# Gated-delta group loop and mixture of experts: diagonal blocks gathered by ACT, whole-tile transposes, the last two norms ahead of the group border, routing weights split by expert

## The chip, the core and the metric

The kernel runs on one core of one Trainium2 chip, in one launch. The metric is the device time of that launch in microseconds, the median of several runs. Five engines work side by side, each through its own list of instructions in order, and wait for one another only at semaphores: PE (TensorE, matmuls), DVE (VectorE), ACT (ScalarE), POOL (GpSimd) and SP (which only issues DMA).

## The reference, cut to what matters

The reference is a two-layer network on `x` of shape (4, 256, 256): per layer a gated mixer and a mixture of experts (MoE), each added to `x`. The change touches the delta-rule attention of the first layer and the way in which the MoE weighs its experts. For each head of the attention a strictly lower triangular matrix is built, the unit triangular system is solved, and the output is normalized and gated:

```python
diff = jnp.where(lower, g[..., :, None] - g[..., None, :], 0.0)
decay = jnp.where(lower, jnp.exp(diff), 0.0)
A = jnp.where(strict, -(k_beta @ jnp.swapaxes(k, -1, -2)) * decay, 0.0)
attn = jax.scipy.linalg.solve_triangular(eyeC - A, eyeC, lower=True, unit_diagonal=True)
...
out = core * jax.lax.rsqrt(jnp.mean(core * core, -1, keepdims=True) + EPS) * norm_w
out = out * jax.nn.silu(z.astype(jnp.float32))
return out.reshape(Bb, Ss, VAL_DIM) @ w_out
```

The first MoE has 64 experts with 64 hidden units each, of which a token takes 6, and one shared expert; the second has 8 experts with 256 hidden units, of which a token takes 2:

```python
h = relu2(jnp.einsum('th,eih->tei', x, w1)) * w_dense[:, :, None]
routed = jnp.einsum('tei,ehi->th', h, w2)
```

## The kernel before

Five phases follow one another: a front phase (gates), `delta_phase`, `moe_phase` 0, a small mixer, `moe_phase` 1. All tokens (1024) lie along the free dimension.

`delta_phase` works through 8 groups (`NG`) of 2 key heads and 4 value heads. `groups` writes group 0 and group 7 out and runs groups 1 to 6 in a hardware loop (`Fori`), on each engine. In what follows g0 is the first group. Nothing but the order of the code and the semaphores decides what runs when; there is no scheduler. One group is, on PE:

1. The border. `gram(g, 0)`, then `rms(g - 1, 6)`, `gram(g, 1)`, `rms(g - 1, 7)`: products of keys and queries of the new group, with the last two norm sums of the group before between them. The matmul of `rms` (L469) goes to ACT's `root` (Ln L797, then Exp L799), then DVE's `normalize` (L970), then POOL's multiply (L1091). The first `gram` waits for the sixth `normalize`.
2. The m stage. Eight steps n of `gram` (L487, L488) and `decay` (L499 to L504). ACT takes the decays into one of two buffers `dec` (L786, L787), DVE multiplies them into `m` (L986, L990). `output` (L477, pairs of matmuls of the group before) is done one pair a step from n = 4 on, the rest behind.
3. `gate` (L518), `turn_v` (L512), and four `project_qk` (L445) of the next group, as cover. Meanwhile DVE copies and transposes the 32x32 diagonal blocks of `m` into `mt`, in four instructions of 32 partitions each (L1002), inverts all blocks by 31 steps of substitution (L1016, L1021), with `add_output` (L950) in between, and then transposes the inverse `inv` into two layouts, `t64` (`untransposed`, L1026) and `pT` (`transposed`, L1031), in seven instructions of 32 partitions. `tr_ready` counts them.
4. `below32` (L526) and `merge32` (L537, L539) build the 64x64 inverses from the 32x32 ones, with ACT's evictions (L849, L854 to L856) between; `filler(4)` is a projection (L445) that waits for the first `convolve` (L942) of DVE, which stands behind the transposes; then the step to 128 (`below64`, `merge64`: L546, L550), `solve` and `cross` (L555, L561).
5. The mix stage. Eight steps of `mix` (L570, L572), `project_v` (L445) and `rms`; two of them also hold `k_norm` (L462), the norm of the next group's keys, which ACT's `root_k` takes (L765).

In `moe_phase` the hidden units are worked in units of 128 by 512: PE `hidden` (L1475), ACT relu, POOL square, PE `weights` (L1485, L1487: spreads the routing weight of an expert over the rows of its hidden units), DVE multiply (L1453), PE `second` (L1495). The routing weights are split in three bf16 parts, so that 3 x 64 = 192 rows do not fit in the 128 rows of one matmul: in MoE 0 `weights` is two matmuls, of 128 rows (parts 0 and 1, `wTa`) and of 64 rows (part 2, `wTb`). DVE also works in these stretches on gates that are needed later (`late_gates`).

## Time and profile before

| | |
|---|---|
| median of 3 runs | 1879.65 us (1879.03 to 1881.52) |
| profiled execution, its own time | 1879.69 us |
| its span, first to last instruction | 1877.8 us |
| mean granted TensorE clock | 0.919 |
| PE busy, share of the span | 1549.9 us, 83% |
| DVE busy, share of the span | 1216.3 us, 65% |
| ACT busy, share of the span | 767.8 us, 41% |
| POOL busy, share of the span | 331.8 us, 18% |

So 1.9 us lie outside the span. Busy times are sums over stages with different limits; what counts at a place is which wait ends last there. The granted clock is 1.0 at 2.4 GHz and 0.5 at 1.2 GHz.

### The profile page before, as it was taken

To read this page: it belongs to the slowest core of one execution; us is meant where nothing else is said; L and a number is where in the kernel's file an instruction comes from. 1 tells how busy PE (TensorE), PEld (TensorE's weight loads), DVE (VectorE), ACT (ScalarE), POOL (GpSimd) and SP (SyncE) were. 2 spreads that over 40 slices of the span, in tenths; PEclk is the share of its full clock that TensorE was granted. 3 is DMA by queue.
4 is the path that set the end of the run, shared out by engine and by line. 5 is a ranking of instruction groups with operands and counts; after the bars stand their busy time and mean duration, and the time that the engine had idled before them with its cause. 6 is when DMAs were issued, how large, how long until landed. Compare 5 with 4: busy or idle time off the path is not lost. (4 is left out here: it accounts for less than half of the span.)

```text
span 1877.8 us, 24845 instructions
## 1 busy us (share of the span) xinstructions
PE 1549.9 (83%) x8568; PEld 870.9 (46%) x8568; DVE 1216.3 (65%) x2045; ACT 767.8 (41%) x1576; POOL 331.8 (18%) x289
## 2 busy tenths in 40 slices
PE   0117869889879889888898898897799999989998
PEld 0113456456447447446446446546433333334433
DVE  6977776785696696596597597585276665632211
ACT  2214545556546555455555564555321111120111
POOL 6110003102102201300300300300322232200222
PEclk9968979979889988898898997997899999989999
DMA  1010000000000000000000000000200111010010
GB/s 56 0 47 23 12 13 13 22 13 12 24 12 12 24 12 12 24 12 13 24 1 13 35 1 13 12 1 13 78 28 28 42 42 42 28 56 24 24 34 35
DMA packets 15815, 43.73 MB, mean 23 GB/s; under 512 B 3344, under 2 KB 6992, under 8 KB 14544
## 3 DMA queue, kind: packets, MB, share of 16 engines
q1 hardware_dynamic: 15696, 42.12, 6.6%
q8 instruction: 77, 1.26, 0.3%
q14 instruction: 42, 0.34, 0.1%
HBM read 40.02 MB, written 2.10 MB: 22 GB/s over the span
## 5 line engine op out<-in xcount | busy, mean ns | idle before, releaser
L942 DVE SCALAR_TENSOR_TENSOR conv<-bank,taps,conv 128x510 f32<-128x510 f32 (+2 forms) x384 | 282.1, 744 | 108.6 <-ACT conv L749 99.0
L445 PE MATMUL bank<-rT,wf 128*128 128x512 f32 x512 | 254.5, 631 | 61.7 <-DMA wf<-in_wf_dram 33.2
L1086 POOL TENSOR_TENSOR sq<-sq,qsq 128x512 f32<-128x512 f32 x64 | 81.4, 1271 | 836.9 <-ACT sq L889 836.9
L1495 PE MATMUL bank<-ffn_weighted,ffn_chunk 128*128 128x512 f32 x400 | 196.9, 616 | 0.0
L1337 ACT ACTIVATE ffn_relu<-bank 128x512 f32<-128x512 f32 x100 | 59.7, 597 | 330.6 <-PE bank L1475 330.6
L1475 PE MATMUL bank<-rT,ffn_chunk 128*128 128x512 f32 x400 | 192.7, 606 | 0.0
L1453 DVE TENSOR_TENSOR ffn_weighted<-ffn_relu,bank 128x512 f32<-128x512 f32 x96 | 65.8, 688 | 186.4 <-POOL ffn_relu L1308 182.2
L749 ACT ACTIVATE conv<-bank,taps 128x512 f32<-128x512 f32 x128 | 88.8, 714 | 187.6 <-PE bank L445 187.6
L445 PEld LDWEIGHTS bank<-rT,wf 128*128 128x128 f32 x512 | 94.4, 201 | 150.8 <-issue 113.7
L1308 POOL TENSOR_TENSOR ffn_relu<-ffn_relu 128x512 f32<-128x512 f32 x96 | 100.6, 1048 | 281.4 <-ACT ffn_relu L1337 281.4
L986 DVE SCALAR_TENSOR_TENSOR m<-bank,ccol,tmp 128x512 f32<-128x512 f32 x128 | 95.3, 745 | 81.0 <-ACT tmp L787 81.0
L1475 PEld LDWEIGHTS bank<-rT,ffn_chunk 128*128 128x128 f32 x400 | 77.6, 195 | 97.4 <-issue 97.4
L477 PE MATMUL bank<-zs,wo 128*128 128x512 f32 x256 | 116.2, 598 | 0.0
L487 PE MATMUL bank<-feat 128*128 128x512 f32 x128 | 83.6, 740 | 38.7 <-issue 15.7
L1091 POOL TENSOR_TENSOR zs<-zs,rs 128x512 f32<-128x512 f32 x64 | 81.3, 1272 | 186.5 <-DVE rs L970 186.5
L518 PE MATMUL bank<-rT,wz 128*128 128x512 f32 x256 | 111.2, 592 | 3.0 <-DVE m L990 3.0
L1495 PEld LDWEIGHTS bank<-ffn_weighted,ffn_chunk 128*128 128x128 f32 x400 | 68.4, 189 | 72.5 <-issue 72.0
L786 ACT ACTIVATE tmp<-bank,gcol 128x256 f32<-128x256 f32 x128 | 60.8, 475 | 81.0 <-PE bank L504 67.5
L1016 DVE TENSOR_TENSOR tmp<-mt,rs 128x31 f32<-128x31 f32 (+15 forms) x248 | 84.8, 342 | 9.1
L1021 DVE TENSOR_TENSOR rs<-rs,tmp 128x31 f32<-128x31 f32 (+15 forms) x248 | 84.8, 342 | 7.5
L469 PE MATMUL bank<-sq,ones 128*128 128x512 f32 x128 | 71.0, 638 | 15.4 <-ACT ln_k L765 11.2
L518 PEld LDWEIGHTS bank<-rT,wz 128*128 128x128 f32 x256 | 48.6, 190 | 63.9 <-issue 63.2
(247 smaller groups left out, 2775.5 us busy)
## 6 DMA issues: line engine op xcount, KB each, us to landing
ffn_chunk<-in_L_chunks_dram SPq DMA_DIRECT2D x25, 512.0 KB, 3.3
wf<-in_wf_dram SPq DMA_DIRECT2D x8, 1024.0 KB, 6.2
wz<-in_wz_dram SPq DMA_DIRECT2D x8, 512.0 KB, 3.3
wo<-in_wo_dram SPq DMA_DIRECT2D x8, 512.0 KB, 3.3
ffn_spread<-in_L_spread_dram SPq DMA_DIRECT2D x17, 128.0 KB, 3.2
side<-in_fT_dram SPq DMA_DIRECT2D x1, 1024.0 KB, 5.0
xT<-in_xT_dram SPq DMA_DIRECT2D x1, 1024.0 KB, 8.5
gate_dram<-gate SPq DMA_DIRECT2D x1, 1024.0 KB, 3.9
```

The lines of the kernel that those rows point to most:

```text
L445: last = pe.matmul(banks[b][:], wf[:, c, n // NH, :], rT[:, c, halves(n % NH)], start=(c == 0), stop=(c == CT - 1))
L477: ins = pe.matmul(banks[b][:], wo[:, v, c * P:(c + 1) * P], zs[:, v, halves(h)], start=(v == 0), stop=(v == GV - 1))
L487: pe.matmul(banks[b0][:], feat[:, 2 * kh + 1, t0:t1], qk[:, :, t0:t0 + T], start=True, stop=True)
L518: last = pe.matmul(banks[n % 4][:], wz[:, c, v, :], rT[:, c, halves(h)], start=(c == 0), stop=(c == CT - 1))
L749: act.activation(conv[:, n % HF, :], banks[b][:], ACT.Copy, scale=taps[:, n // NH, KS - 1:KS]).then_inc(conv0_ready, 1)
L942: dve.scalar_tensor_tensor(acc[:, :, k:], src[:, :, 0:T - k], taps[:, n // NH, KS - 1 - k:KS - k], acc[:, :, k:], ALU.mult, ALU.add).then_inc(
L986: dve.scalar_tensor_tensor(to[:, 0:2 * T].rearrange("p (a i) -> p a i", a=2), banks[b0][:].rearrange("p (a i) -> p a i", a=2), ccol[:, v, ...
L1016: dve.tensor_tensor(t, mt[:, j, j + 1:].unsqueeze(2).to_broadcast([P, n, j + 1]), inv[:, j, 0:j + 1].unsqueeze(1).to_broadcast([P, n, j + ...
L1021: dve.tensor_tensor(below, below, t, ALU.subtract).then_inc(inv_step, 1)
L1308: pool.tensor_tensor(h2[:, slot, :], hr[:, slot, :], hr[:, slot, :], ALU.mult).then_inc(square_done, 1)
L1475: last = pe.matmul(banks[h][:], chunk[:, slot, c, t * P:(t + 1) * P], rT[:, c, halves(h)], start=(c == 0), stop=(c == CT - 1))
L1495: last = pe.matmul(banks[4 + 2 * c + h][:], chunk[:, slot, CT + t, c * P:(c + 1) * P], hw[:, u, :], start=start, stop=stop, skip_group_che ...
```

## The change

It has five parts, and the numbers of arithmetic results are the same.

- **Blocks and transposes.** ACT gathers the diagonal blocks out of `m` into one whole tile `blocks` (a view of `sq`), in 12 copies (`take_blocks`: four after the sixth decay step, four of them after the eighth, four when `m` is complete). DVE then transposes it in one instruction of 128 partitions, and likewise the inverse in two (`invU`, `invT`), in place of 4 + 7 instructions of 32 partitions. `below32` and `merge32` read `invU` and `invT` directly. Two copies of ACT put two of the blocks into `t64`, and four of POOL put the blocks into `pT`.
- **Decay buffers.** `dec` has four buffers in place of two, so ACT waits for DVE's product of four steps back.
- **Border.** `rms` 6 and 7 and their `root` stand at the end of the group, ahead of the border and of the loop's branch; `normalize` 6 and 7 stand before the m stage of DVE. `output` starts at n = 1. One `add_output` stands before the transposes.
- **Keys' norm.** `k_norm` 0 and 1 stand one and three steps earlier in the mix stage, and ACT's `square_k`, `root_k` with them.
- **Routing weights by expert.** In MoE 0 the 64 experts are split in 40 and 24. Each chunk needs the weights of one side only, all three parts of them: 3 x 40 = 120 rows or 3 x 24 = 72. `weights` is one matmul a unit. The spread matrix of a chunk is loaded by three DMAs in place of one, and the loops are cut where the side changes. MoE 1 is as it was.

```diff
-TURNS = 7
+TURNS = 2
+BLOCKS = 12
...
-    dec = tmp[:, 0:6 * P].rearrange("p (r x) -> p r x", r=2)
+    dec = [t[:, r * 3 * P:(r + 1) * 3 * P] for t in (tmp[:], qsq[:].rearrange("p k x -> p (k x)")) for r in range(2)]
...
+    blocks = sq[:].rearrange("p n x -> p (n x)")[:, 0:SB * SB].rearrange("p (n i) -> p n i", n=PAIRS * 2)
+    invT, invU = blocks, tmp[:].rearrange("p (n c) -> p n c", n=PAIRS * 2)
...
@@ tensor, group @@
             gram(g, 0)
-            if not first:
-                pe.wait_ge(ln_done, before - 3)
-                rms(g - 1, 6)
             pe.wait_ge(conv_ready, (g + 1) * NF * NH)
             gram(g, 1)
-            if not first:
-                pe.wait_ge(ln_done, before - 2)
-                rms(g - 1, 7)
...
-            for n in range(2, GK * B):
-                pe.wait_ge(m_ready, g * PAIRS + 2 * n - 2)
-                gram(g, n)
-                decay(g, n)
-                if not first and n >= 4:
-                    if n == 4:
+            for n in range(1, GK * B):
+                if n >= 2:
+                    pe.wait_ge(m_ready, g * PAIRS + 2 * n - 2)
+                    gram(g, n)
+                    decay(g, n)
+                if not first:
+                    if n == 1:
                         pe.wait_ge(og_ready, before - 1)
-                    output(g - 1, 0, 4, n - 4)
+                    if n == 5:
+                        pe.wait_ge(og_ready, before)
+                    output(g - 1, (n - 1) // 4, 4 + (n - 1) // 4, (n - 1) % 4)
...
-            pe.wait_ge(tr_ready, g * TURNS + 2)
+            pe.wait_ge(tr_ready, g * TURNS + 1)
...
-            pe.wait_ge(tr_ready, g * TURNS + 4)
+            pe.wait_ge(tr_ready, g * TURNS + 2)
...
-            pe.wait_ge(tr_ready, g * TURNS + 6)
+            pe.wait_ge(t64_set, (g + 1) * 2)
+            pe.wait_ge(placed, g * 4 + 2)
...
-            pe.wait_ge(tr_ready, g * TURNS + 7)
+            pe.wait_ge(placed, g * 4 + 4)
...
                 mix(g, n)
                 if not last_group:
+                    if n == 3:
+                        pe.wait_ge(conv_ready, p * NF * NH + 6)
+                        k_norm(p, 1)
                     project_v(p, n)
+                    if n == 1:
+                        pe.wait_ge(conv_ready, p * NF * NH + 5)
+                        k_norm(p, 0)
...
+            for n in (NU - 2, NU - 1):
+                pe.wait_ge(ln_done, g * NU + n - 1)
+                rms(g, n)
@@ scalar @@
+        def take_blocks(g, kh, seqs, after):
+
+            act.wait_ge(m_ready, g * PAIRS + after)
+            t0, t1 = 2 * seqs[0], 2 * seqs[-1] + 2
+            for q in range(4):
+                r = slice(q * SB, (q + 1) * SB)
+                to = blocks[r, :, :].rearrange("p (v t) i -> p v t i", v=GV)
+                of = by_tile[r, :, :, 2 * P + q * SB:2 * P + (q + 1) * SB].rearrange("p (v s) t i -> p v (s t) i", v=GV)
+                act.activation(to[:, 2 * kh:2 * kh + 2, t0:t1, :], of[:, 2 * kh:2 * kh + 2, t0:t1, :],
+                               ACT.Copy).then_inc(blocks_ready, 1)
...
             for n in range(GK * B):
                 decays(g, first, n)
+                if n == 5:
+                    take_blocks(g, 0, range(0, 4), 8)
+            take_blocks(g, 1, range(0, 2), 12)
+            take_blocks(g, 1, range(2, 4), 16)
...
+            act.wait_ge(tr_ready, g * TURNS + 1)
+            for q in range(2):
+                r = slice(q * SB, (q + 1) * SB)
+                act.activation(t64[r, :, r], invU[r, :, :], ACT.Copy).then_inc(t64_set, 1)
@@ vector, group @@
+            if not first:
+                add_output(g - 1, 0, 4)
+            dve.wait_ge(blocks_ready, (g + 1) * BLOCKS)
+            dve.transpose(mt[:].rearrange("p j i -> p i j"), blocks.rearrange("p n i -> p i n")).then_inc(mt_ready, 1)
...
+            dve.transpose(invU.rearrange("p n c -> p c n"), inv.rearrange("p i c -> p c i")).then_inc(tr_ready, 1)
+            dve.transpose(invT.rearrange("p n i -> p i n"), inv).then_inc(tr_ready, 1)
@@ gpsimd, group @@
+            pool.wait_ge(tr_ready, (g + 1) * TURNS)
+            pool.wait_ge(zeroed, 2)
+            pool.sem_inc(pool_passed, 1)
+            for q in (2, 3, 0, 1):
+                r = slice(q * SB, (q + 1) * SB)
+                pool.tensor_copy(pT[r, :, r], invT[r, :, :]).then_inc(placed, 1)
@@ moe_phase @@
-    KA = 3 * E if 3 * E <= P else 2 * E
-    KB = 3 * E - KA
+    EA = E if 3 * E <= P else 40
+    KA, KB = 3 * EA, 3 * (E - EA)
...
-            last = pe.matmul(banks[2 + h][:], spreadb[:, slot, at], wTa[:, halves(h)], start=True, stop=not KB)
-            if KB:
-                last = pe.matmul(banks[2 + h][:], spreadb[0:KB, slot, at], wTb[:, halves(h)], start=False, stop=True)
-            last.then_inc(spread_full, 1)
+            rows, of = (KB, wTb) if low else (KA, wTa)
+            pe.matmul(banks[2 + h][:], spreadb[0:rows, slot, at], of[:, halves(h)], start=True, stop=True)\
+              .then_inc(spread_full, 1)
```

The order of PE's instructions at the end of a group inside the loop, before the change: L570 and L572 are `mix`, L445 `project_v`, L469 `rms`, L413 the loop's branch, L487 and L488 `gram`, L499 the first `decay`.

```order
L445 MATMUL bank<-rT,wf 128x512 x2
L711 REGISTER_ALU
L469 MATMUL bank<-sq,ones 128x512
L413 REGISTER_ALU
L413 COMPARE_AND_BRANCH
L487 MATMUL bank<-feat 128x512
L488 MATMUL bank<-feat 128x256
L469 MATMUL bank<-sq,ones 128x512
L487 MATMUL bank<-feat 128x512
L488 MATMUL bank<-feat 128x256
L469 MATMUL bank<-sq,ones 128x512
L499 MATMUL bank<-rows,sel 128x256
```

The same place of the changed kernel, where `rms` is L475, `gram` L493 and L494, `decay` L505:

```order
L451 MATMUL bank<-rT,wf 128x512 x2
L475 MATMUL bank<-sq,ones 128x512 x3
L419 REGISTER_ALU
L419 COMPARE_AND_BRANCH
L493 MATMUL bank<-feat 128x512
L494 MATMUL bank<-feat 128x256
L493 MATMUL bank<-feat 128x512
L494 MATMUL bank<-feat 128x256
L505 MATMUL bank<-rows,sel 128x256
```

The two norm sums have gone from between the `gram`s to the end of the group, ahead of the branch. DVE's instructions around the end of the inversion, before (L1026 and L1031 are the transposes, L942 the first convolution):

```order
L1021 TENSOR_TENSOR rs<-rs,tmp 128x31
L1037 REGISTER_ALU
L1026 STREAM_TRANSPOSE t<-rs 32x32x32 x2
L1031 STREAM_TRANSPOSE pT<-rs 32x32x32 x2
L1026 STREAM_TRANSPOSE t<-rs 32x32x32
L1031 STREAM_TRANSPOSE pT<-rs 32x32x32 x2
```

And now (`tmp` holds `invU`, `sq` holds `invT`):

```order
L1034 TENSOR_TENSOR rs<-rs,tmp 128x31
L1041 REGISTER_ALU
L1042 STREAM_TRANSPOSE tmp<-rs 128x32x32
L1043 STREAM_TRANSPOSE sq<-rs 128x32x32
L951 REGISTER_ALU
```

Seven instructions of 32 partitions have become two of 128. PE's instructions of two units of MoE 0 in the loop, before:

```order
L1475 MATMUL bank<-rT,ffn_chunk 128x512 x2
L1485 MATMUL bank<-ffn_weights_t,ffn_spreadb 128x512
L1487 MATMUL bank<-ffn_weights_t_low,ffn_spreadb 128x512
L1495 MATMUL bank<-ffn_weighted,ffn_chunk 128x512 x2
L1475 MATMUL bank<-rT,ffn_chunk 128x512 x2
```

And now:

```order
L1498 MATMUL bank<-rT,ffn_chunk 128x512 x2
L1509 MATMUL bank<-ffn_weights_t,ffn_spreadb 128x512
L1517 MATMUL bank<-ffn_weighted,ffn_chunk 128x512 x2
L1498 MATMUL bank<-rT,ffn_chunk 128x512 x2
```

One matmul a unit has gone; nothing else has moved there.

## Rows read from the trace of the kernel before

**Rows 1.** The page: the granted clock in 40 slices of the span.

```profile
PEclk9968979979889988898898997997899999989999
```

**Rows 2.** Timeline of PE, border g1 to g2: start, us, instruction [idle before].

```profile
474.00 1.13 PE L469 MATMUL bank<-sq,ones 128*128 128x512 f32 x2 [0.94 <-ACT ln_k L765]
479.68 2.07 PE L487 MATMUL bank<-feat 128*128 128x512 f32 x2 [4.56 <-issue]
...
487.68 0.27 PE L499 MATMUL bank<-rows,sel 96*128 96x256 bf16 x1 [0.87 <-ACT rs L797]
```

**Rows 3.** Timeline of PE, border g6 to g7, outside the loop.

```profile
1207.91 1.13 PE L469 MATMUL bank<-sq,ones 128*128 128x512 f32 x2 [0.94 <-ACT ln_k L765]
...
1218.57 0.27 PE L499 MATMUL bank<-rows,sel 96*128 96x256 bf16 x1 [0.93 <-ACT rs L797]
```

**Rows 4.** Timeline of PE, m stage and outputs of g2.

```profile
491.17 1.57 PE L487 MATMUL bank<-feat 128*128 128x512 f32 x2 [1.15 <-DVE m L990]
...
501.90 1.08 PE L477 MATMUL bank<-zs,wo 128*128 128x512 f32 x2
...
507.43 11.38 PE L477 MATMUL bank<-zs,wo 128*128 128x512 f32 x26
518.64 1.88 PE L518 MATMUL bank<-rT,wz 128*128 128x512 f32 x4
```

**Rows 5.** Timeline of DVE, inversion of g2.

```profile
510.34 8.68 DVE L1002 STREAM_TRANSPOSE mt<-m 32x1024 f32<-32x1024 f32 x4
...
519.25 0.69 DVE L950 TENSOR_TENSOR xT<-xT,bank 128x512 f32<-128x512 f32 x1
...
544.39 3.86 DVE L1026 STREAM_TRANSPOSE t<-rs 32x1024 f32<-32x1024 f32 x2
...
557.88 2.23 DVE L942 SCALAR_TENSOR_TENSOR conv<-bank,taps,conv 128x510 f32<-128x510 f32 x3
```

**Rows 6.** Timeline of PE, middle of g2.

```profile
548.40 2.73 PE L526 MATMUL bank<-t,m 32*32 32x32 f32 x128 [3.43 <-DVE t L1026]
...
560.16 3.57 PE L445 MATMUL bank<-rT,wf 128*128 128x512 f32 x4 [3.14 <-DVE conv L942]
```

**Rows 7.** A window of it: busy us of PE, PEld, DVE, ACT, POOL, granted clock.

```profile
549.72:563.40 13.68, 8.50 (x253) 6.07 (x245) 13.38 (x13) 5.56 (x15) 0.00 (x0) 0.50 0.01 2
```

**Rows 8.** Timeline of PE: `below32` of g0 and of g7.

```profile
252.80 1.40 PE L526 MATMUL bank<-t,m 32*32 32x32 f32 x45 [9.69 <-DVE t L1026]
...
1280.16 3.62 PE L526 MATMUL bank<-t,m 32*32 32x32 f32 x128 [10.46 <-DVE t L1026]
```

**Rows 9.** Groups by line and shape: busy us, mean ns of one.

```profile
L1002 DVE STREAM_TRANSPOSE mt<-m 32x1024 f32<-32x1024 f32 x32 | 69.0, 2158 | 0.6
L849 ACT ACTIVATE mt<-bank 128x256 f32<-128x256 f32 x32 | 12.3, 384 | 50.2 <-PE bank L526 50.0
...
L856 ACT ACTIVATE pT<-bank 32x256 f32<-32x256 f32 x32 | 12.0, 375 | 0.4
```

**Rows 10.** Timeline of ACT, start of MoE 0: two operations of 1024 elements.

```profile
1345.05 2.00 ACT L1340 ACTIVATE ffn_sig<-xT 128x1024 f32<-128x1024 f32 x2 [11.80 <-DVEq L1686]
```

**Rows 11.** Timeline of PE: a unit of MoE 0, and one of MoE 1.

```profile
1510.42 0.38 PE L1485 MATMUL bank<-ffn_weights_t,ffn_spreadb 128*128 128x512 bf16 x1
...
1514.58 0.38 PE L1485 MATMUL bank<-ffn_weights_t,ffn_spreadb 128*128 128x512 bf16 x1
...
1754.53 0.38 PE L1485 MATMUL bank<-ffn_weights_t,ffn_spreadb 24*128 24x512 bf16 x1
...
1758.48 0.39 PE L1485 MATMUL bank<-ffn_weights_t,ffn_spreadb 24*128 24x512 bf16 x1
```

**Rows 12.** Timeline of POOL and DVE in MoE 0: the same copy twice, other neighbours.

```profile
1508.54 0.69 DVE L1205 TENSOR_TENSOR late_fwd_num<-late_fwd_num,late_ownv 128x512 f32<-128x512 f32 x1
1508.60 0.88 POOL L1318 CAST ffn_spreadb<-ffn_spread 128x256 bf16<-128x256 f32 x1 [0.38 <-DMA ffn_spread<-in_L_spread_dram]
...
1525.28 0.40 POOL L1318 CAST ffn_spreadb<-ffn_spread 128x256 bf16<-128x256 f32 x1 [0.45 <-DMA ffn_spread<-in_L_spread_dram]
```

More of the change, by code:

```diff
@@ L994, in group @@
                        .then_inc(m_ready, 1)
[L995 to L1006 removed]
+            if not first:
+                add_output(g - 1, 0, 4)
+            dve.wait_ge(blocks_ready, (g + 1) * BLOCKS)
+            dve.transpose(mt[:].rearrange("p j i -> p i j"), blocks.rearrange("p n i -> p i n")).then_inc(mt_ready, 1)
+            adds = {} if first else {0: (1, 5), 6: (2, 6), 12: (3, 7)}
             dve.wait_ge(inv_set, g + 1)
@@ L1477, in hidden, with weights @@
             last.then_inc(hidden_full, 1)
-        def weights(n, u, slot):
+        def weights(n, u, slot, low=False):
             if not (isinstance(n, int) and n < UNWEIGHTED + 2):
@@ L1507, in turn @@
                     hidden(c * 4 + u, u, slot)
-                weights(c * 4 + u, u, slot)
+                weights(c * 4 + u, u, slot, low)
                 if u >= 2:
```

166 lines of the change are left out of this document (77 added, 89 removed).

## The prediction

> **What bounds the kernel now.** I read the page first, then the timeline of PE, keeping the rows with an idle entry, then DVE's and ACT's timelines at those places. PE is busy 83% of the span, and the clock dips in two of every four slices of the group loop [rows 1]. The chain of waits at the end of the run is PE in the MoE, one matmul behind the other; there only fewer matmuls help. In the group loop PE waits in four places of each group, and these waits are the room for the change:
>
> - The border: from the end of `project_v` (the start of rms minus its wait, 473.06) to the first decay at 487.68 PE needs 14.6 us [rows 2]. In the four other turns of the loop it is 12.2, 14.4, 12.4 and 12.6, and outside the loop 11.6 (1206.97 to 1218.57) [rows 3]; the mean of the seven is 12.8.
> - The m stage and the outputs: 27.5 us from 491.17 to 518.64 [rows 4].
> - The middle: `below32` waits 3.43 us for DVE's transposes, `filler(4)` 3.14 us for the first convolution, queued behind seven transposes [rows 6]. From `below32` to `filler(4)` it is 11.76 us, within 0.02 in all seven groups that have a filler.
> - One wait of 0.94 us for `root_k` in the mix stage, like the one in [rows 2].
>
> Without cover, in g0 and g7, `below32` waits 9.69 and 10.46 us [rows 8]: there DVE's chain itself is the path.
>
> **DVE's chain.** In [rows 5] the transposes into `mt` cost 8.68 us, one add 0.69, and the two transposes that `below32` waits for 3.86. I price a whole-tile transpose by the row of 32 partitions, 2.16 us for `mt` [rows 9] and 1.93 for the others, since what counts elsewhere in this trace is the number of elements along the free dimension: ACT's copies of 256 elements take 0.375 on 32 partitions and 0.384 on 128 [rows 9]. The unknown is whether 128 partitions cost more: below, the row of 32 cannot be undercut by more than its whole 1.9; above, four blocks of 32 in turn make 8.7 and 7.7. I take the low row. ACT's last four copies of the blocks come after `m` is complete, 4 x 0.384 [rows 9] plus 0.2 to wake, 1.75 us; the other eight lie in ACT's idle time of the m stage. So `mt` takes 3.9 in place of 8.7 (-4.8), one add moves ahead into that wait (-0.7), `invU` is one transpose in place of two (-1.9): 7.4 us less. The Trainium skill, "Vector Engine (DVE) Microarchitecture Reference", section on the reshape front-end, says that a transpose sustains one element per cycle per lane. For 1024 elements that would be an estimated 1.1 us; no row here shows it, the trace has 1.9 to 2.2, and I stay with the trace. By that figure the sum would be smaller by some 5 us, in g0 and g7 alone.
>
> **The m stage, g1 to g7.** One step with one pair of outputs takes (507.43 - 501.90) / 2 = 2.77 us, a pair 11.2 / 13 = 0.86, so a step alone 1.90. Six steps and 16 pairs need 25.2 of the 27.5 us; one pair now lies in the wait of 1.15 [rows 4]. That is room for 3.1; some 0.7 of it was lost to the half clock behind the border, and I leave that in: 2.4. PE reached `below32` 57.3 us after the first decay (548.40 - 3.43 - 487.68), and now after 54.9; DVE had it ready after 60.7, and now after 53.3. So PE no longer waits: `below32` starts 60.7 - 54.9 = 5.8 us earlier, x 6 (g1 to g6) = **35**. In g7 DVE decides: **7.4**. In g0, without outputs, a step takes 2.5 us, as ACT waits for DVE with two buffers; with four it is DVE's 2.1, 2.8 over the stage, and the chain lacks the add: 2.8 + 6.7 = **9.5**.
>
> **From `below32` to `filler(4)`.** The seven transposes no longer stand before the convolution, which is ready 4.2 us after `invU`. New is that ACT must put `t64` right before its first eviction: two copies of 1024 elements, 1.0 us each by [rows 10], behind the tap of the fourth projection. First eviction 3.3 us after `below32` starts (0.7 tap, 2.0, 0.4, latencies), then `merge32`, 4.7 us: 8.1 in place of 11.76, 3.65 us, x 6 = **21.9**. In g0 ACT has long been idle: **4.5**. In g7 the same copies lie open but the last transposes go: **2**. POOL's four copies into `pT` are on no path: by the cast of 256 elements at 0.40 [rows 12], 1.6 each and 6.4 together, against 8.7 us until `merge64` needs two and 16 until `solve` needs four. The same cast took 0.88 beside a DVE operation with both inputs in SBUF [rows 12]. The Trainium skill, "SBUF — State Buffer", section on who interferes with whom, has this as a lock: such a DVE operation and a POOL operation that reads SBUF exclude one another. DVE's convolutions at that time read a PSUM bank, so by that rule too the copies stay at the low price; at 0.88 x 4 = 3.5 each they would take 14 and still fit.
>
> **The border.** `project_v` ends, three norm sums of 0.86 follow without the 0.94, then the loop's branch. In the loop PE restarts 4.4 to 5.7 us after the last norm sum before the branch began (5.68 in [rows 2]), so the first `gram` comes at 6.1 to 7.4, then 2.6 to 4.1 of `gram`s: the first decay at 8.7 to 11.5, in place of 13.2. ACT's three roots end at 5.0 and do not hold it, and DVE's two `normalize` end before the first decay is through. I take 3.3 us, x 7 = **23**; bounds 12 and 33. The 0.94 in the mix stage goes as well, x 7 = **6.6**: `root_k` comes three steps earlier, right behind its matmuls.
>
> **MoE 0.** A unit takes 4.16 us with two `weights` matmuls, in MoE 1 with one 3.95 [rows 11]. PE runs without a gap in both. 64 weighted units x 0.21 = **13.5**, less 0.3 for six copies of weights in place of three. DVE had its product done 5.7 us before PE needed it, POOL's cast of the spread rows has 2 us in hand against 1.0 for two more DMA issues.
>
> **Sum.** 35 + 7.4 + 9.5 + 21.9 + 4.5 + 2 + 23 + 6.6 + 13.3 = 123.2. From the profiled execution's 1879.7, which is the median of the runs (1879.65): **1756**.
>
> **The clock.** The middle of g2 ran at 0.50, that is 1.2 GHz, for 13.7 us [rows 7], from shortly after the wait for `below32` on; `filler(4)` took 3.57 in it where others take 1.88. I kept this cost, since the small matmuls of `below32` and `merge32` alone did not bring the clock back there. The Trainium skill, "TensorE: Matmul & The Clock Gate", section on the clock gate, puts the fall down to idle time of PE; then the middle would stay at 2.4 GHz once the wait is gone, some 2.2 us a group, 15 in all.
>
> **Rivals.**
> - *More than that* (chance 0.2): the middle keeps 2.4 GHz, or the border gives its upper bound: 1722 to 1742.
> - *The wait moves to ACT* (0.2): ACT's copies for `t64` and the blocks, and the loop's branch, eat half of the gain of the middle and of the border (13 + 12), and more small waits appear: 1770 to 1795. For it: ACT works without a break before both places. Against: it is busy 41%.
> - *A transpose costs by its blocks of 32 partitions* (0.03): then `mt` is as before plus 1.75, `invU` 3.9 longer, `invT` 7.7: `below32` 5.0 us later, `filler(4)` 0.8 more, 46 in all over eight groups, against 43 from border, norm and MoE: 1883, slower than before. It decides from about 5.5 us more for each transpose. Against it: ACT's rows of 32 and of 128 partitions.
> - *POOL's copies hold `merge64` and `solve`* (0.03): slower from 8 us a copy; at the worst row, 2.5 for 1024 elements, nothing.
> - *The second matmul of `weights` was hidden* (0.04): 1770. Against: the two units of [rows 11].
> - The forecast itself, 1742 to 1770: 0.5.
>
> **Numbers.** The range of 8 in 10 takes in most of the first two rivals: 1730 to 1788. A change under 0.2% cannot be told from none. Faster 0.94, same 0.03, slower 0.03.
>
> **What would show it.** Whole-tile transposes of 1.9 to 2.2 us; no wait before `below32` in g1 to g6; `filler(4)` about 8 us after it; groups 133 us apart instead of 147; a unit of MoE 0 at 3.95; the first decay 10 us after `project_v`. I am wrong if a transpose of 128 partitions costs several times that row, if PE waits for `placed` or for ACT's `t64`, or if restarting after the branch costs as much more as the norm sums gave.

## The result, and the profile after

The changed kernel takes **1760.29 us** (median of 4 runs, 1755.2 to 1761.61) against 1880.03 of the kernel before in the same comparison: a ratio of 0.9352, 95% interval 0.9335 to 0.9368, faster by 120 us. The forecast was 1756, range 1730 to 1788. The total came out in part by luck: several of its terms did not, and large errors of opposite sign hid each other. So the experiments below are mostly about the terms.

The table compares the two profiled executions (1877.8 and 1758.1 us of span) stretch by stretch along TensorE. A stretch runs from the start of one landmark to the start of the next (the end of `project_v` is, as in the prediction, the start of the norm sum behind it less that one's wait); each cell sums the groups named.

| stretch | groups | before, us | after, us | gain |
|---|---|---|---|---|
| border: end of `project_v` to first decay | g1 to g7 | 89.3 | 79.1 | 10.2 |
| first decay to first gate (m stage, outputs) | g1 to g7 | 219.8 | 195.9 | 23.8 |
| the same | g0 | 20.9 | 23.5 | -2.6 (1.7 of it not the change's, see e9) |
| first gate to `below32` | g1 to g7 | 208.4 | 183.0 | 25.3 |
| the same | g0 | 36.0 | 29.2 | 6.8 |
| `below32` to `filler(4)` | g0 to g6 | 82.3 | 65.5 | 16.8 |
| `filler(4)` to the first mix | g0 to g6 | 193.4 | 188.6 | 4.8 |
| first mix to the end of `project_v` | g0 to g6 | 234.2 | 224.6 | 9.6 |
| `below32` to the first mix | g7 | 29.2 | 30.0 | -0.8 |
| weights transposes to the mixer's first matmul (MoE 0) | | 275.2 | 247.1 | 28.1 |

That is 122.0; the first decay of g0 came 2.5 us later in the profiled execution after, which leaves 119.5 of the 119.7 by which the spans differ. (Over the other executions profiled, that first decay stands anywhere from 196 to 199 us, so the 2.5 is no part of the change.)

The page's clock line after, to be read against [rows 1]: from g1 on the group loop has two slices left under nine tenths. The dips are shorter, not gone, as the windows further down show.

```profile
PEclk9977889999999999998999998997899999998999
```

Groups of instructions after, with count, busy us, mean ns and idle time before them, against [rows 5, 9, 10, 12]. The transposes of all 128 partitions cost what those of 32 did:

```profile
L1105 POOL COPY pT<-sq 32x1024 f32<-32x1024 f32 x32 | 33.0, 1033 | 495.6 <-DVE sq L1043 494.2
L796 ACT ACTIVATE sq<-m 32x256 f32<-32x256 f32 x64 | 26.4, 412 | 5.2 <-DVE m L1007 4.0
L859 ACT ACTIVATE t<-tmp 32x1024 f32<-32x1024 f32 x16 | 16.8, 1049 | 2.8 <-DVE tmp L1042 2.6
L1042 DVE STREAM_TRANSPOSE tmp<-rs 128x1024 f32<-128x1024 f32 x8 | 15.9, 1985 | 1.0 <-DVE rs L1034 0.8
L1017 DVE STREAM_TRANSPOSE mt<-sq 128x1024 f32<-128x1024 f32 x8 | 15.7, 1968 | 10.2 <-ACT sq L796 10.2
```

The middle of g3, timeline of PE (start, us, operation, idle before it), against [rows 6]. `below32` (L532) has no wait any more. `merge32` (L543, L545) waits 1.15 us for ACT's eviction, stands still twice more with nothing named, and `filler(4)` (L451) follows 9.6 us after `below32` in place of 11.76:

```profile
652.09 2.21 PE L532 MATMUL bank<-tmp,m 32*32 32x32 f32 x128
...
655.46 0.22 PE L543 MATMUL bank<-sq,mt 32*32 32x32 f32 x2 [1.15 <-ACT mt L863]
...
657.45 0.26 PE L545 MATMUL bank<-mt,sq 32*32 32x32 f32 x1 [0.99 <-issue]
...
661.34 0.26 PE L545 MATMUL bank<-mt,sq 32*32 32x32 f32 x1 [1.39 <-issue]
...
661.64 2.93 PE L451 MATMUL bank<-rT,wf 128*128 128x512 f32 x3
```

Two windows of it, the columns of [rows 7]. The clock still falls to 0.50, 4 us after `below32` began, though the wait of 3.4 us ahead of it is gone; it stays there for 10.2 us, where it was 13.7 in g2 of before and 20.5 in g3:

```profile
652.09:656.05 3.96, 2.81 (x180) 2.72 (x180) 3.89 (x5) 3.80 (x7) 2.27 (x3) 1.00 0.45 139
656.05:666.30 10.25, 7.88 (x168) 5.01 (x158) 6.06 (x10) 5.43 (x15) 1.86 (x2) 0.50 0.01 2
```

The whole way from `below32` to the first mix of g3, before and after. In g1 to g6 the mean clock of this stretch was 0.75 to 0.82 before and is 0.82 to 0.90 after; the time at 0.50 fell from 106 to 58 us:

```profile
693.12:733.38 40.26, 35.49 (x560) 29.44 (x561) 27.15 (x30) 19.84 (x40) 0.00 (x0) 0.75 0.02 8
652.09:688.42 36.33, 32.26 (x561) 26.16 (x561) 19.13 (x26) 22.20 (x43) 4.13 (x4) 0.86 0.06 17
```

A border inside the loop (g2 to g3), timeline of PE and then of DVE, against [rows 2]: `project_v` ends at 583.95, the three norm sums follow, the last of them after a wait of 0.85 us for POOL's square, then both engines stand for over 4.5 us with no releaser named ("issue"), and the first `gram` runs at half clock.

```profile
583.95 1.88 PE L475 MATMUL bank<-sq,ones 128*128 128x512 f32 x4
586.68 1.10 PE L475 MATMUL bank<-sq,ones 128*128 128x512 f32 x2 [0.85 <-POOL sq L1084]
592.55 2.07 PE L493 MATMUL bank<-feat 128*128 128x512 f32 x2 [4.77 <-issue]
```

```profile
592.51 0.18 DVE L944 COPY taps<-taps_all 128x32 f32 x1 [4.56 <-issue]
```

The border to g7, outside the loop, against [rows 3]: the same work, no stop, full clock, 6.7 us from `project_v` to the first decay.

```profile
1127.76 1.88 PE L475 MATMUL bank<-sq,ones 128*128 128x512 f32 x4
1130.49 1.10 PE L475 MATMUL bank<-sq,ones 128*128 128x512 f32 x2 [0.85 <-POOL sq L1084]
1131.79 1.10 PE L493 MATMUL bank<-feat 128*128 128x512 f32 x2 [0.21 <-DVE rs L984]
...
1134.45 0.28 PE L505 MATMUL bank<-rows,sel 96*128 96x256 bf16 x1
```

Units of MoE 0 and of MoE 1 after, timeline of PE, against [rows 11]. MoE 0 now repeats every 3.65 us, faster than MoE 1 with its 3.95, from which the forecast had taken the unit to come. Read from start to start, the `weights` matmul holds PE for 0.22 us with 120 rows and 0.31 to 0.32 with 24 rows, the four matmuls behind it (L1517) for 1.72 and 1.82, and the four ahead of it (L1498) for 1.72 and 1.81.

```profile
1303.19 0.38 PE L1509 MATMUL bank<-ffn_weights_t,ffn_spreadb 120*128 120x512 bf16 x1
1303.41 1.88 PE L1517 MATMUL bank<-ffn_weighted,ffn_chunk 128*128 128x512 f32 x4
1305.12 1.88 PE L1498 MATMUL bank<-rT,ffn_chunk 128*128 128x512 f32 x4
1306.84 0.38 PE L1509 MATMUL bank<-ffn_weights_t,ffn_spreadb 120*128 120x512 bf16 x1
...
1662.51 0.39 PE L1509 MATMUL bank<-ffn_weights_t,ffn_spreadb 24*128 24x512 bf16 x1
1662.83 1.98 PE L1517 MATMUL bank<-ffn_weighted,ffn_chunk 128*128 128x512 f32 x4
1664.65 1.88 PE L1498 MATMUL bank<-rT,ffn_chunk 128*128 128x512 f32 x4
1666.46 0.38 PE L1509 MATMUL bank<-ffn_weights_t,ffn_spreadb 24*128 24x512 bf16 x1
```

### The profile page after: what moved, and what is told of

Same layout as the page of the kernel before. It is cut to its first block and busy times, and to the rows that moved or that the text cites. A ratio compares the mean times of both kernels' runs of the same rounds, so it can differ in the third digit from the quotient of the medians.

```text
span 1758.1 us, 24833 instructions
## 1 busy us (share of the span) xinstructions
PE 1492.6 (85%) x8504; PEld 852.1 (48%) x8504; DVE 1105.3 (63%) x1984; ACT 821.1 (47%) x1688; POOL 369.9 (21%) x321
## 5 line engine op out<-in xcount | busy, mean ns | idle before, releaser
L451 PE MATMUL bank<-rT,wf 128*128 128x512 f32 x512 | 255.8, 634 | 40.9 <-DMA wf<-in_wf_dram 33.1
L1498 PE MATMUL bank<-rT,ffn_chunk 128*128 128x512 f32 x400 | 193.1, 607 | 0.0
L1517 PE MATMUL bank<-ffn_weighted,ffn_chunk 128*128 128x512 f32 x400 | 190.7, 600 | 1.8 <-DVE ffn_weighted L1476 1.8
L1330 POOL TENSOR_TENSOR ffn_relu<-ffn_relu 128x512 f32<-128x512 f32 x96 | 107.0, 1115 | 245.9 <-ACT ffn_relu L1359 245.9
L451 PEld LDWEIGHTS bank<-rT,wf 128*128 128x128 f32 x512 | 94.9, 202 | 129.9 <-issue 114.7
L1105 POOL COPY pT<-sq 32x1024 f32<-32x1024 f32 x32 | 33.0, 1033 | 495.6 <-DVE sq L1043 494.2
L1498 PEld LDWEIGHTS bank<-rT,ffn_chunk 128*128 128x128 f32 x400 | 77.8, 195 | 97.7 <-issue 97.5
L483 PE MATMUL bank<-zs,wo 128*128 128x512 f32 x256 | 121.1, 604 | 0.0
L1517 PEld LDWEIGHTS bank<-ffn_weighted,ffn_chunk 128*128 128x128 f32 x400 | 73.3, 189 | 82.8 <-issue 73.2
L493 PE MATMUL bank<-feat 128*128 128x512 f32 x128 | 78.6, 700 | 26.3 <-issue 21.7
L1048 DVE TENSOR_TENSOR z<-z,bank 128x512 f32<-128x512 f32 x32 | 22.0, 688 | 102.0 <-PE bank L567 102.0
L1003 DVE SCALAR_TENSOR_TENSOR m<-bank,ccol,tmp 128x512 f32<-128x512 f32 x64 | 47.8, 747 | 53.4 <-ACT tmp L785 51.8
```

Of the source, the lines that this page charges most:

```text
L451: last = pe.matmul(banks[b][:], wf[:, c, n // NH, :], rT[:, c, halves(n % NH)], start=(c == 0), stop=(c == CT - 1))
L483: ins = pe.matmul(banks[b][:], wo[:, v, c * P:(c + 1) * P], zs[:, v, halves(h)], start=(v == 0), stop=(v == GV - 1))
L1330: pool.tensor_tensor(h2[:, slot, :], hr[:, slot, :], hr[:, slot, :], ALU.mult).then_inc(square_done, 1)
L1498: last = pe.matmul(banks[h][:], chunk[:, slot, c, t * P:(t + 1) * P], rT[:, c, halves(h)], start=(c == 0), stop=(c == CT - 1))
L1517: last = pe.matmul(banks[4 + 2 * c + h][:], chunk[:, slot, CT + t, c * P:(c + 1) * P], hw[:, u, :], start=start, stop=stop, skip_group_che ...
```

## The experiments

Each ratio is to the kernel before, timed on the same chip. A difference to the changed kernel is the difference of the two ratios times 1880 us; with the two intervals it is uncertain by some 5 us.

| kernel | us | ratio, 95% interval |
|---|---|---|
| changed kernel | 1760.3 | 0.9352, 0.9335 to 0.9368 |
| e1 before, MoE part alone | 1852.2 | 0.9845, 0.9818 to 0.9873 |
| e2 norm sums back | 1756.8 | 0.9342, 0.9318 to 0.9367 |
| e3 k_norm back | 1767.4 | 0.9389, 0.9367 to 0.9411 |
| e4 groups written out on TensorE | 1735.5 | 0.9233, 0.9204 to 0.9262 |
| e5 MoE 1 padded | 1751.2 | 0.9304, 0.9281 to 0.9327 |
| e6 before, low part padded | 1861.7 | 0.9898, 0.9878 to 0.9917 |
| e7 groups written out on all engines | 1720.8 | 0.9151, 0.9128 to 0.9174 |
| e8 t64 by POOL | 1761.4 | 0.9365, 0.9348 to 0.9382 |
| e9 transposes back | 1822.3 | 0.9684, 0.9660 to 0.9708 |
| e10 outputs back | 1781.7 | 0.9461, 0.9438 to 0.9485 |
| e11 filler(4) first | 1761.9 | 0.9350, 0.9293 to 0.9407 |
| e12 e7 and e5 together | 1706.0 | 0.9059, 0.9036 to 0.9081 |

### The MoE part: e1, e6, e5

**e1.** The kernel before with the changed `moe_phase` (its part of the diff shown ahead, from `EA` to `turn(..., low)`) and nothing else.

> The kernel before with only the MoE part of the change (routing weights laid out by expert, one weights matmul per unit in place of two). The prediction's term: 64 units x 0.21 us less 0.3, so 13.3 us less than before, about 1866, and a unit of MoE 0 at 3.95 us. Rival (the second matmul was hidden behind other work of the unit): no gain, 1880, and a unit stays at 4.16. A second rival: the three DMA issues per chunk in place of one and the six copies of weights eat part of it: 5 to 10 us.

Measured: 29 us less (24 to 34 by the interval), twice the term, and the unit at 3.65, not 3.95. All three expectations missed. A unit lost 0.51 us, more than the 0.21 at which the missing matmul was priced, and MoE 1's 3.95 is no floor. What the two slow units share is a `weights` matmul with few rows: 64 in MoE 0 before, 24 in MoE 1. That gave the theory of the next two.

**e6.** The kernel before, the low part of 64 rows filled up with 32 rows of zeros.

```
-wTb = sb("weights_t_low", [max(KB, 1), NT], BF16)
+wTb = sb("weights_t_low", [96 if KB else 1, NT], BF16)
+        pool.memset(wTb[64:96, :], 0.0).then_inc(padded, 1)
...
-    last = pe.matmul(banks[2 + h][:], spreadb[0:KB, slot, at], wTb[:, halves(h)], start=False, stop=True)
+    last = pe.matmul(banks[2 + h][:], spreadb[0:96, slot, at], wTb[:, halves(h)], start=False, stop=True)
```

> The kernel before; in MoE 0 the second weights matmul of each unit gets 96 rows in place of 64 (32 of them zeros), and computes the same. Theory of the switch: both matmuls fall from 0.31 to 0.22 and the matmul behind them loses 0.1, so a unit comes from 4.16 to about 3.87, and 64 units save 19 us of the 29 that the MoE part of the change gave: 1861. Rival (the 29 us came from the fewer matmuls and their issue alone): no change, 1880.

Measured: 19 us less (1 - 0.9898 = 0.0102), as the theory said; 32 more rows of zeros make the program faster. Timeline of PE, one unit: both `weights` matmuls (L1489 with 128 rows, L1491 now with 96) hold PE for 0.21 and 0.22 us, where they held it for 0.31 and 0.32, and the four behind them take 1.72, not 1.82: 0.3 us a unit, 19 in 64 units.

```profile
1404.41 0.38 PE L1489 MATMUL bank<-ffn_weights_t,ffn_spreadb 128*128 128x512 bf16 x1
1404.62 0.38 PE L1491 MATMUL bank<-ffn_weights_t_low,ffn_spreadb 96*128 96x512 bf16 x1
1404.84 1.88 PE L1499 MATMUL bank<-ffn_weighted,ffn_chunk 128*128 128x512 f32 x4
1406.56 1.88 PE L1479 MATMUL bank<-rT,ffn_chunk 128*128 128x512 f32 x4
```

**e5.** The changed kernel, MoE 1's 24 rows filled up to 96 in the same way.

```
+    KM = KA if KB else 96
+        if not KB:
+            pool.memset(spreadb[:], 0.0).then_inc(padded, 1)
+            pool.memset(wTa[:], 0.0).then_inc(padded, 1)
...
-            rows, of = (KB, wTb) if low else (KA, wTa)
+            rows, of = (KB, wTb) if low else (KM, wTa)
```

> The changed kernel; in MoE 1 the operands of the weights matmul (24 rows) get 72 more rows of zeros, so that it has 96 rows and computes the same. Theory (a matmul of 64 rows or fewer between matmuls of 128 rows costs TensorE a switch before and after it): a unit of MoE 1 comes from 3.95 us to the 3.65 that MoE 0 has with 120 and 72 rows, 32 units x 0.30 = 9.6 us, 1751, and the matmul itself from 0.31 to 0.22. Rival (the 0.3 us come from MoE 1's other layout or data, not from the rows): no change, 1760 plus 1 or 2 us for setting the zeros.

Measured: 9 us less (0.9352 - 0.9304), and the unit of MoE 1 at 3.65 (1660.08 to 1663.73), as in MoE 0:

```profile
1660.08 0.38 PE L1517 MATMUL bank<-ffn_weights_t,ffn_spreadb 96*128 96x512 bf16 x1
1660.30 1.88 PE L1525 MATMUL bank<-ffn_weighted,ffn_chunk 128*128 128x512 f32 x4
1662.01 1.88 PE L1506 MATMUL bank<-rT,ffn_chunk 128*128 128x512 f32 x4
1663.73 0.38 PE L1517 MATMUL bank<-ffn_weights_t,ffn_spreadb 96*128 96x512 bf16 x1
```

So a matmul of 24 or 64 rows between matmuls of 128 rows costs about 0.3 us in all: 0.1 on the matmul ahead of it, 0.1 on itself and 0.1 on those behind. Of the MoE part's 29 us, 19 are this price and 10 the missing matmul (64 x 0.22 = 14) less some 4 us around the units, which were not taken apart. The Trainium skill, "TensorEngine Tiling (Array Packing)", section on the tiling modes, has the array run in modes of 128, 64 or 32 rows and says that changing the mode drains the engine; the runs agree, and put the price here at 0.3 us for the two changes, into the other mode and back. Where the threshold between 64 and 72 rows lies they do not show.

### The border: e2, e3, e4, e7

**e2.** The changed kernel, norm sums 6 and 7, their roots and waits back behind the next group's grams.

```
             gram(g, 0)
+            if not first:
+                pe.wait_ge(ln_done, before - 3)
+                rms(g - 1, 6)
...
             gram(g, 1)
+            if not first:
+                pe.wait_ge(ln_done, before - 2)
+                rms(g - 1, 7)
```

> The changed kernel with the last two norm sums (and their roots) put back among the first grams of the next group; all else as changed. The prediction's term for this part is 23 us (3.3 for each of seven borders), so 1783. Theory now, from the two traces: inside the loop the move gains almost nothing (13.6 us from project_v to the first decay before, 13.1 after), since PE stands still for 4.1 to 4.8 us at the loop's branch whatever lies ahead of it, and only the two borders outside the loop gain 5.0 us each: 12 us, so 1772. Rival: the move costs or gains elsewhere (DVE's normalize now lies ahead of the first step), then neither.

Measured: 2 us less than the changed kernel, not told apart from it, and surely not 12 more. (By the rows the border inside the loop was 13.2 us before, not 13.6.) On top of the moved `k_norm`, moving the norm sums brought nothing.

**e3.** The changed kernel with `k_norm`, `root_k` and `square_k` at their old steps.

```
-                    if n == 3:
-                        pe.wait_ge(conv_ready, p * NF * NH + 6)
-                        k_norm(p, 1)
                     project_v(p, n)
...
+                if not last_group and n == 6:
+                    pe.wait_ge(ln_done, g * NU + 4)
+                    k_norm(p, 1)
```

> The changed kernel with k_norm, its roots and its squares at their old places of the mix stage; all else as changed. The prediction's term is 6.6 us (a wait of 0.94 us in each of seven groups), so 1767. From the traces the mix stage became 1.2 us shorter in each of seven groups, 8.4 in all: 1769. Rival: the wait only hid another wait of the border, and it makes no difference: 1760.

Measured: 7 us more (0.9389 - 0.9352), the term of 6.6; the mix stage is 1.4 us longer in each of the seven groups. With e2 and e3 beside before and after, the border can be read as a square (us from `project_v` to the first decay, means):

| | inside the loop (5) | outside (2) | all seven |
|---|---|---|---|
| before | 13.2 | 11.6 | 89 |
| only norm sums moved (e3) | 12.6 | 7.1 | 77 |
| only `k_norm` moved (e2) | 10.9 | 10.3 | 75 |
| both (after) | 13.1 | 6.7 | 79 |

Either move alone shortens the border; and the norm sums moved on top of `k_norm` lengthen it by 4 us over the seven. Inside the loop the norm sums ahead of the branch even cost 2.3 us a turn: in e2 PE stood 2.92 us there, waiting for DVE's `normalize` and as long as outside the loop (2.98 and 3.02), in after 4.1 to 4.8 with nothing named. So a wait that is needed anyway can cover the branch. These are single executions, in which the borders inside the loop lie up to 2.9 us apart, and the total of e2 does not show the 4 us.

**e4.** The changed kernel, TensorE's middle groups written out.

```
-        with eng.Fori(1, NG - 1) as g:
-            group(g, False, False)
+        if 'tensor.' in group.__qualname__:
+            for g in range(1, NG - 1):
+                group(g, False, False)
+        else:
+            with eng.Fori(1, NG - 1) as g:
+                group(g, False, False)
```

> The changed kernel with the six middle groups written out one after the other on TensorE, in place of a loop; the other engines keep their loops. Theory (TensorE's restart over the loop's branch sets the border): the five borders inside the loop come from 13.1 us towards the 6.7 us of the two outside it: up to 5 x 6.4 = 32 us less than the changed kernel, 1728. Rival 1 (another engine's loop branch, DVE's of 2.8 us or ACT's, sets it): the gain is under 2 us a border, 1750 to 1760. Rival 2 (a longer program costs TensorE more in fetching instructions everywhere): slower than the changed kernel, over 1765.

Measured: 22 us less by the ratios, 25 by the medians. Every border is 6.7 us, as the theory said, and a third of that comes back later: from the first decay to the first gate it is 27.9 us in g1 and 30.0 to 31.0 in g2 to g6. DVE, still in its loop, is what PE now waits for. Timelines of PE and of DVE at the border g2 to g3:

```profile
575.53 1.10 PE L479 MATMUL bank<-sq,ones 128*128 128x512 f32 x2 [0.84 <-POOL sq L1088]
576.85 1.10 PE L497 MATMUL bank<-feat 128*128 128x512 f32 x2 [0.22 <-DVE rs L988]
...
581.77 0.28 PE L509 MATMUL bank<-rows,sel 96*128 96x256 bf16 x1 [1.54 <-ACT tmp L789]
```

```profile
581.27 0.18 DVE L948 COPY taps<-taps_all 128x32 f32 x1 [4.47 <-issue]
```

**e7.** The same on every engine (`for g in range(1, NG - 1)` in place of the loop).

> The changed kernel with the six middle groups written out on all engines. With TensorE alone written out the border was 6.7 us everywhere, and the stretch from the first decay to the first gate grew from 27.9 to 30.2, since DVE restarts 4.5 us after its last operation of the group. Theory (that growth is DVE's own branch): it goes back to 27.9, 5 x 2.3 = 11.5 us less than with TensorE alone, 1724. Rival (four longer programs cost instruction fetches on every engine): 1735 or more.

Measured: 38 us less than the changed kernel and 15 less than e4. The border is 6.7 to 6.8 and the stretch behind it 28.0 to 28.1 in g1 to g7. So a turn of the loop cost TensorE and DVE together 6.4 us at the border, five times over: 32 us. Another 9 us went between `below32` and `filler(4)`: in g1, g3 and g4 the last of the nameless stops in `merge32` is missing and `filler(4)` follows after 6.6 to 7.1 us, in no group of after in less than 8.7. So writing out changed these stops too; why is open. The Trainium skill, "Advanced Engine Details and Errata", section on control flow timing, has 0.05 to 0.11 us for a branch; over this loop's back edge the trace of after shows 4.1 to 4.8 on TensorE. The two queues that the page calls "instruction" moved fewer packets once the groups were written out (page of after, then of e7), so the longer program fetched less, not more:

```profile
q8 instruction: 78, 1.28, 0.3%
q14 instruction: 68, 0.56, 0.1%
```

```profile
q8 instruction: 65, 1.06, 0.3%
q14 instruction: 33, 0.27, 0.1%
```

That a jump back makes the engine fetch its instructions anew, and that this is the stop, fits these lines; it was not measured by itself.

### The middle: e9, e10, e8, e11

**e9.** The changed kernel with DVE's eleven transposes of 32 partitions, and without ACT's and POOL's copies of blocks.

```
-            dve.wait_ge(blocks_ready, (g + 1) * BLOCKS)
-            dve.transpose(mt[:].rearrange("p j i -> p i j"), blocks.rearrange("p n i -> p i n")).then_inc(mt_ready, 1)
+            dve.wait_ge(m_ready, (g + 1) * PAIRS)
+            for q in range(4):
+                r = slice(q * SB, (q + 1) * SB)
+                last = dve.transpose(mt[r, :, :].rearrange("p j i -> p i j"), ...)
+            last.then_inc(mt_ready, 1)
...
-            dve.transpose(invU.rearrange("p n c -> p c n"), inv.rearrange("p i c -> p c i")).then_inc(tr_ready, 1)
-            dve.transpose(invT.rearrange("p n i -> p i n"), inv).then_inc(tr_ready, 1)
+            untransposed(0); untransposed(2); transposed(1); transposed(3); untransposed(1); transposed(2); transposed(0)
```

> The changed kernel with DVE's transposes as before: four of 32 partitions into mt, seven into t64 and pT, and no copies of blocks by ACT or POOL; the early outputs, the four dec buffers, the moved k_norm and norm sums and the MoE part stay. By the prediction's terms DVE is then ready for below32 some 60 us after the first decay in place of 53, while TensorE comes after 54: a wait of 6 us in g1 to g6, 7.4 in g7, 6.7 in g0, and filler(4) comes 11.8 us after below32 in place of 9.3, 15 in seven groups: 36 + 14 + 15 = 65 us more, 1825. Rival (POOL's and ACT's new copies cost elsewhere what the transposes gave): under 1800.

Measured: 62 us more (0.9684 - 0.9352), 65 expected. The wait of 6 us before `below32` is there, then `filler(4)` 11.7 us behind it:

```profile
680.55 3.63 PE L532 MATMUL bank<-t,m 32*32 32x32 f32 x128 [5.94 <-DVE t L1035]
```

One stretch is better than in after: from the first decay to the first gate of g0, 20.9 us against 23.5. It is also just what it was before, although e9 has the four `dec` buffers: they gave nothing in g0. PE still waits for `m` ahead of every second step, and two steps take 5.0 us, before and in e9 (PE, g0; first before, then e9):

```profile
204.55 1.13 PE L487 MATMUL bank<-feat 128*128 128x512 f32 x2 [0.80 <-DVE m L990]
...
209.57 1.12 PE L487 MATMUL bank<-feat 128*128 128x512 f32 x2 [0.80 <-DVE m L990]
```

```profile
206.09 1.12 PE L493 MATMUL bank<-feat 128*128 128x512 f32 x2 [0.80 <-DVE m L999]
...
211.10 1.12 PE L493 MATMUL bank<-feat 128*128 128x512 f32 x2 [0.80 <-DVE m L999]
```

What after has more there is ACT's copies of blocks, which in g0 have no outputs to hide behind: 2.56 us of them between two decays (in after at 214.06). DVE's product behind them starts 0.9 us late (DVE, g0; first e9, then after):

```profile
213.87 0.75 DVE L995 SCALAR_TENSOR_TENSOR m<-bank,ccol,tmp 128x512 f32<-128x512 f32 x1 [0.72 <-ACT tmp L784]
```

```profile
217.49 0.75 DVE L1003 SCALAR_TENSOR_TENSOR m<-bank,ccol,tmp 128x512 f32<-128x512 f32 x1 [1.63 <-PE bank L494]
```

The other 1.7 us are no part of the change. In the profiled execution of after the clock stood at 0.50 from 202.1 to 205.5, in the middle of this stretch. In e8 and e11, whose code is the same up to there, it did not, and the stretch took 21.8. The code of before shows the same pair: 20.9, and 22.6 in e1.

**e10.** The changed kernel with the outputs as before, the first from the fifth step on.

```
-                if not first:
-                    if n == 1:
-                        pe.wait_ge(og_ready, before - 1)
-                    if n == 5:
-                        pe.wait_ge(og_ready, before)
-                    output(g - 1, (n - 1) // 4, 4 + (n - 1) // 4, (n - 1) % 4)
+                if not first and n >= 4:
+                    if n == 4:
+                        pe.wait_ge(og_ready, before - 1)
+                    output(g - 1, 0, 4, n - 4)
```

> The changed kernel with the outputs of the group before at their old places of the m stage (from the fifth step on, the second set behind the last step); all else as changed. By the traces the stretch from the first decay to the first gate fell from 31.4 to 28.0 us; if the earlier outputs gave that, it goes back by 3 us or so in seven groups: 21 to 24 more, 1782. Rival (the four dec buffers and the norm sums moved ahead gave it, and the outputs fill no wait): under 1767. Rival 2: DVE's chain, which no longer waits for these outputs, hides them: no change.

Measured: 20 us more by the ratios, 21 by the medians. The stretch goes back to 29.8 to 31.7 us in all seven groups, and nothing behind it takes it up except in g7 (22.9 in place of 25.5). So the m stage's gain is the outputs', and the four `dec` buffers show no gain of their own in g1 to g7, as in g0 (e9).

**e8.** The changed kernel, the two copies into `t64` moved from ACT to POOL.

```
-            act.wait_ge(tr_ready, g * TURNS + 1)
-            for q in range(2):
-                act.activation(t64[r, :, r], invU[r, :, :], ACT.Copy).then_inc(t64_set, 1)
...
+            pool.wait_ge(tr_ready, g * TURNS + 1)
+            for q in range(2):
+                pool.tensor_copy(t64[r, :, r], invU[r, :, :]).then_inc(t64_set, 1)
```

> The changed kernel with the two copies of inverse blocks into t64 made by POOL (ahead of its four copies into pT) in place of ACT. Theory (ACT's 2.1 us for them hold merge32 back by the 1.15 us that TensorE waits there, and by more in the evictions behind): filler(4) comes 7.3 to 8.2 us after below32 in place of 9.3, so 1 to 2 us a group, 8 to 16 in all: 1744 to 1752. Rival (merge32 would then wait for DVE's second transpose, and the wait only moves): no change. Rival 2 (POOL's six copies come too late for merge64): slower.

Measured: no change. The wait for ACT is gone from `merge32`, but PE stands there all the same, with nothing named, and longer than the 0.99 us of after:

```profile
652.65 0.25 PE L545 MATMUL bank<-mt,sq 32*32 32x32 f32 x1 [1.59 <-issue]
```

My theory, that ACT's 2.1 us held the middle, falls. `filler(4)` follows 8.5 to 9.3 us after `below32`, as in after. What makes these two stops stayed open; in e7 the second of them is missing in three groups. POOL did six copies of 1.03 to 1.08 us here without holding anything.

**e11.** The changed kernel, `filler(4)` ahead of `merge32`.

```
                 below32(v)
+            filler(4)
             pe.wait_ge(tr_ready, g * TURNS + 2)
...
                 merge32(v)
-            filler(4)
```

> The changed kernel with filler(4), four matmuls of 512 columns, between below32 and merge32 instead of behind merge32, and ACT's tap of it likewise. Theory (the middle falls to 1.2 GHz because TensorE does hundreds of 32x32 matmuls there with small stops between them): the clock stays longer at 2.4 GHz, filler(4) takes 1.9 us in place of 3.4, and the middle is 1 to 2 us shorter a group: 1746 to 1753. Rival (the fall comes whatever stands there, or the evictions of merge32, no longer covered by filler(4), lie open): 1760 to 1775.

Measured: 1761.9, with runs from 1747.6 to 1767.6; no gain can be told. In its profiled execution the clock fell 0.3 to 0.7 us after `filler(4)` had begun in g2 to g6, so the four matmuls took 3.2 to 3.5 us, hardly less than before; most of `merge32` ran at full clock, and the clock fell once more before its end. In g1 `filler(4)` ran at full clock, in 1.98 us, and the fall came only in `merge32`, 8.8 us after `below32` began. The time at 0.50 in the middles of g1 to g6 is 58 us, as in after. Windows of PE in g3: busy, clock, DMA.

```profile
652.10:655.62 3.52, 3.52 (x19) 0.52 0.00 0
655.62:658.94 3.32, 2.19 (x180) 1.00 0.02 5
658.94:664.70 5.76, 5.16 (x73) 0.51 0.01 3
```

So four large matmuls behind `below32` do not keep the clock up, though in g1 the fall came later. That the small matmuls and not the wait make it fall is neither shown nor excluded: what stood ahead of the first fall in g2 to g6 was `below32` and a stop of 1.3 us, and the second came in `merge32`, beside a stop of 1.7 to 2.3 us.

**e12.** e7 and e5 together.

> The changed kernel with both parts that gained: the six middle groups written out on all engines, and the weights matmul of MoE 1 with 96 rows. If the two gains add up (39 and 9 us), 1711. Rival (the longer program slows the MoE's loops, or the padding's gain was of that chip alone): 1717 to 1721.

Measured: 1706.0, a ratio of 0.9059, 55 us less than the changed kernel, where e7 and e5 gave 38 and 9; they add up, and what is over them is about the uncertainty. This version beats both kernels.

## Why the prediction was right in sum

By its own terms, forecast and measured:

| step | forecast | measured | by |
|---|---|---|---|
| `below32` earlier, g1 to g6 | 35 | 41.1 | stretches; e9, e10 |
| DVE's chain, g7 | 7.4 | 8.1 | stretches |
| g0 | 9.5 | 4.1 | stretches; e9 |
| `below32` to `filler(4)`, g1 to g6 | 21.9 | 15.6 | stretches |
| the same, g0 | 4.5 | 1.2 | stretches |
| g7, behind `below32` | 2 | -0.8 | stretches |
| border | 23 | 10.2 | stretches; e2, e3 |
| `root_k` | 6.6 | 9.6 | stretches; e3 (7 in time) |
| MoE 0 | 13.3 | 28.1 | stretches; e1 |
| not in the sum: `filler(4)` to mix | 0 | 4.8 | stretches |

- **Price of a whole-tile transpose.** Right: 1.93 to 1.99 us against 1.93 and 2.16 taken from rows of 32 partitions. This carried the argument, and the rival on the other side (blocks in turn, 1883) is out. The figure of the Trainium skill ("Vector Engine (DVE) Microarchitecture Reference", section on the reshape front-end), which gave an estimated 1.1, is not what these 24 instructions show.
- **PE instead of DVE decides at `below32`.** Right. Forecast 54.9 us after the first decay, measured 54.2 (27.9 + 26.3). No wait remains in g1 to g6. The 0.7 us per group that I had left in for the half clock went as well.
- **`below32` to `filler(4)`: 8.1 forecast, 8.7 to 9.5 measured.** The first eviction came as worked out (3.37 us after `below32`, forecast 3.3). The term that was off is `merge32`, 4.7 forecast, 6.2 measured in g3 with its two nameless stops; e8 shows that ACT is not their cause.
- **g0: two steps failed.** "With four it is DVE's 2.1, 2.8 over the stage": e9 has the four buffers and no copies by ACT, and a step still takes 2.5 us, because PE waits 0.80 us for `m` ahead of every second step, a wait that the change left as it was. It was not ACT's wait for a buffer that set the step; the term is nothing. And "the other eight lie in ACT's idle time of the m stage" is true for g1 to g7 (27.9 us in after and in e9), false for g0, whose steps have no outputs: 0.9 us. The chain's part was right, 6.8 for 6.7. The last 1.7 us are the clock of the profiled execution.
- **Border: the step "I take 3.3 us, x 7" failed.** Forecast 23, measured 10.2, below the lower bound of 12. Outside the loop the move gave more than the term, 4.9 us each. Inside it gave 0.1 a turn, which is the warning that the text gave ("if restarting after the branch costs as much more as the norm sums gave"). In the text's own terms: the third norm sum waited 0.85 us for POOL's square, which the text had at nothing; the first `gram` came 7.9 to 8.6 us after `project_v`, not 6.1 to 7.4; and the `gram`s, mostly at half clock, took 4.1 to 5.3, not 2.6 to 4.1. In e2's trace the move of the norm sums is a loss there; e4 and e7 show that the back edge itself is the price.
- **MoE 0: the step "A unit takes 4.16 us with two `weights` matmuls, in MoE 1 with one 3.95" failed.** The two units differ in more than the count: MoE 1's matmul has 24 rows. I compared two rows of the profile that both held the same hidden cost, so it dropped out of the difference; e5 and e6 show it.
- **POOL's copies.** Off the path, as said, at 1.03 us each, not 1.6, none of the 32 over 1.05: a hold-up by DVE, as in [rows 12], shows in none of them. That rival is out.
- **The clock.** The rival that the middle keeps 2.4 GHz once PE no longer waits does not hold as it stands: the clock fell in the middle of every group. But "I kept this cost" is not right either: the time at half clock fell from 106 to 58 us in g1 to g6. The 4.8 us behind `filler(4)`, which the sum had at nothing, are part of that. Behind `filler(4)` of g0 to g6 the clock stood at 0.50 for 46 us before and 35 after, and the stretch to the first mix is 26.1 us with 2.8 us of half clock in it (g1) and 28.5 with 8.7 (g6), 0.4 us more for each; before, it is 26.3 with 3.2 (g2) and 28.5 with 8.7 (g3).
- **The wait moves to ACT.** The sizes of that rival came near (the middle of g1 to g6 and the border gave 19 us less than their terms, 25 in the rival), its mechanism did not: neither shortfall is ACT's (e8 for the middle; at the border PE and DVE stand with nothing named).

## What to carry to other kernels

Compare matmul rows by their row counts before one is taken as the price of another: here one matmul of few rows among full ones also slowed its neighbours, and rows of zeros were the cheapest fix. Work moved ahead of a loop's branch need not be hidden by it: look at the same border inside and outside the loop first, and try writing out a loop of few, long turns before reordering the work around its edge. When a sum comes out right, check its terms one by one; here an error of 15 us, with some smaller ones, hid three of 13, 6 and 5.
